# One attention and mixture-of-experts layer on one core: the map of whole tiles computed between other steps, turned a visit earlier, and ten fill addresses' registers read later

## What is computed

```python
x = L0_attn_x                                        # 32 x 256 x 128
h = _layernorm(x) * (1 + ca) + sa
x = x + ga * attention(h, w_in, b_in, w_out, b_out)  # 16 heads of 8
h = _layernorm(x) * (1 + cb) + sb
logits = h @ router_w                                # 14 experts
assignments = argmax(logits); weights = softmax(logits)[assignments]
hid = gelu(h @ w1[e] + b1[e]); out = hid @ w2[e] + b2[e]   # e = the token's expert
x = x + gb * out * weights
```

## Time and profile before

| | |
|---|---|
| median of the runs before | 603.12 us (three runs: 601.77, 603.12, 1474.33) |
| the profiled execution's own time | 602.05 us |
| its span, first to last instruction | 600.2 us |
| busy share of the span | PE 78%, DVE 92%, ACT 91%, POOL 81% |
| attention part, its drain and the expert part | about 0 to 490, 490 to 506 and 506 to 600 us |

### The profile page before, as it was taken

The page is one execution under the profiler, slowest core; times in us unless marked ns, Lnnn a source line. Parts: engine busy times, 40 slices in busy tenths (PEclk is TensorE's granted clock), DMA queues, the critical chain, the costliest instruction groups (busy, mean ns, idle before and its releaser), DMA issues.

```text
span 600.2 us, 12121 instructions
## 1 busy us (share of the span) xinstructions
PE 466.0 (78%) x2531; PEld 263.6 (44%) x2531; DVE 550.7 (92%) x1398; ACT 547.8 (91%) x2339; POOL 486.1 (81%) x647
## 2 busy tenths in 40 slices
PE   5456878887887887787787888778777677999993
PEld 2112433443443343343343343334333345889992
DVE  5899999999999999999999999999999977888994
ACT  2599999999999999999999999999999996678881
POOL 4566777989899988999999898999888687777773
PEclk9555565556556556756655655675665558999997
DMA  6366455544555554545455555666555513798760
GB/s 197 105 192 160 136 139 134 142 140 138 144 141 142 142 149 141 150 143 156 148 155 146 151 146 154 172 177 170 153 150 163 157 64 125 231 335 245 236 198 27
DMA packets 77080, 94.42 MB, mean 157 GB/s; under 512 B 12814, under 2 KB 60718, under 8 KB 77006
## 3 DMA queue, kind: packets, MB, share of 16 engines
q1 hardware_dynamic: 68850, 75.69, 45.7%
q0 software_dynamic: 6144, 16.82, 7.5%
q10 hardware_dynamic: 2015, 1.15, 0.8%
HBM read 58.41 MB, written 35.20 MB: 156 GB/s over the span
## 4 chain that ended last, share of the span: by engine, by line
ACT 44%; POOL 17%; PE 15%; DVE 8%; issue 7%; SPq 3%; DMA 3%; ACTq 1%; POOLq 0%; DVEq 0%
ACT scores L940 43%; PE scores L1263 5%; PE scores L1254 5%; POOL table L847 3%; DVE neg_max L1423 3%; SPq L592 3%; POOL xhat L792 2%; POOL rstd L775 2%; PE scores L1244 1%; POOL rest L581 1%; POOL parts L584 1%; POOL h_scaled L815 1%; DMA x_s<-table 1%; POOL att L804 1%; DMA more_rooms<-table 1%
## 5 line engine op out<-in xcount | busy, mean ns | idle before, releaser
L940 ACT ACTIVATE scores<-scores,neg_max 128x256 f32<-128x256 f32 x1024 | 467.2, 808 | 10.8 <-DVE neg_max L1423 10.6
L940 ACT ACTIVATION_READ_ACCUMULATOR scores<-scores,neg_max 128x1 f32 x1024 | 419.8, 569 | 0.0
L1423 DVE TENSOR_REDUCE neg_max<-scores 128x4 f32<-128x1024 f32 x256 | 309.3, 1211 | 7.4 <-PE scores L1104 6.8
L1104 PE MATMUL scores<-k_stack,q_stack 64*128 64x256 bf16 x1024 | 148.2, 388 | 79.6 <-ACT scores L940 65.5
L1104 PEld LDWEIGHTS scores<-k_stack,q_stack 64*128 64x128 bf16 x1024 | 34.1, 106 | 163.5 <-ACT scores L940 116.2
L847 POOL DMA_INDIRECT table<-rows,place_i x64 | 66.1, 1034 | 20.6 <-issue 15.2
L792 POOL TENSOR_SCALAR xhat<-rows,mv,rstd 128x128 f32<-128x128 f32 x60 | 47.6, 794 | 6.8 <-POOL rstd L775 6.8
L1263 PE MATMUL scores<-w_s,hid 128*128 x308 | 49.2, 284 | 1.4 <-DVE y_biased_s L1993 1.2
L1132 PE MATMUL side_a<-w_gated,opt_t 128*128 128x128 f32 x128 | 49.8, 491 | 0.0
L784 POOL TENSOR_SCALAR xhat<-x_s,mv,rstd 128x128 f32<-128x128 f32 x62 | 49.0, 798 | 0.4 <-POOL rstd L775 0.4
L906 POOL DMA_INDIRECT out_dram<-x_s x40 | 39.2, 980 | 12.2 <-issue 8.8
(11 more groups left out here) (230 smaller groups left out, 882.1 us busy)
## 6 DMA issues: line engine op xcount, KB each, us to landing
q_stack<-parts_dram SPq DMA_DIRECT2D x192, 64.0 KB, 2.9
x_s<-table SPq DMA_DIRECT2D x62, 192.5 KB
parts_dram<-parts SPq DMA_DIRECT2D x31, 384.0 KB
k_stack<-parts_dram SPq DMA_DIRECT2D x186, 64.0 KB, 2.3
mod_b<-mod_rows SPq DMA_DIRECT2D x32, 256.0 KB, 4.4
x_s<-in_x_dram SPq DMA_DIRECT2D x13, 256.0 KB, 5.1
table<-pad_tile SPq DMA_DIRECT2D x15, 192.5 KB
more_rooms<-table SPq DMA_DIRECT2D x15, 192.5 KB
```

Source lines behind the costliest of these rows:

```text
L940: last = act.activation(buf[:, k * L:k * L + L], buf[:, k * L:k * L + L], ACT.Exp, bias=neg_max[:, p, n:n + 1], accum_out=exp_sum[:, p, n: ...
L1104: last = pe.matmul(scores[:, c, at:at + L], q_stack[p][r, g + j, t * P:t * P + P], k_stack[p][r, g + j, :], start=True, stop=True)
L1423: dve.tensor_reduce(to, scores[:, (PAIRS * b.n + i) % RING, :].rearrange("p (e j m) -> p e j m", e=2, j=2), AX_X, ALU.max, negate=True).th ...
```

## The change

Three things change, and nothing of what is computed.

1. The map's twelve operations are split into functions of their own and stand one by one between the drain's last operations and the first `bias_y`, `gate_y` and `out_y`. Three of them (`map_rows_left`, `map_tiles`, `map_full`) now stand ahead of `bias_y(0)`.
2. `MAP_TURNED` is 7 and not 8: TensorE turns the map at the head of visit 7, and VectorE takes it in its own step 6.
3. SyncE reads the ten addresses of `end_row` behind the loads of visits 14 and 15.

```diff
-MAP_TURNED = 8
+MAP_TURNED = 7
...
                 sp.wait_ge(map_ready, 1)
                 whole_rows.extend(load_many(sp, tile_row, EARLY, whole_reload(EARLY), 0, PAD_AT))
-                ends.extend(load_many(sp, end_row, FILLS_FIRST, E - FILLS_FIRST, 0, PAD_AT))
...
                 sp.dma_start(rows_in[j % ROOMS][:, :], table[ds(row, P), :]).then_inc(rows_loaded[s], 16)
+                if j == FILLS_FROM - 1:
+                    ends.extend(load_many(sp, end_row, FILLS_FIRST, E - FILLS_FIRST, 0, PAD_AT))
...
                 note_ends()
+                map_rows_left()
                 own_place(other)
+                map_tiles()
                 note_place(other)
+                map_full()
                 weigh_last()
-                for n in range(FIRST):
-                    bias_y(n)
-                for n in range(FIRST):
-                    gate_y(n)
-                for n in range(FIRST):
-                    out_y(n)
-                map_counts()
+                bias_y(0)
+                bias_y(1)
+                map_spread()
+                gate_y(0)
+                map_below()
+                gate_y(1)
+                map_upto()
+                out_y(0)
+                map_bases()
+                map_from()
+                out_y(1)
+                map_in()
+                map_pick()
+                map_sums()
+                map_columns()
                 whole_y(FIRST)
-                map_rows()
-                map_columns()
                 bias_y(FIRST + 1)
                 gate_y(FIRST + 1)
```

Each new function holds one operation of the old chain, with a wait on the one that it reads:

```diff
-            def map_counts():
+            def map_rows_left():
 
                 dve.wait_ge(counted, GROUPS)
-                steps.then(dve.tensor_tensor(early_i[:, 0, :], next_row[0:NT, :], sums_of[:, 3, :], ALU.subtract))
...
+                step["left"] = steps.did(dve.tensor_tensor(early_i[:, 0, :], next_row[0:NT, :], sums_of[:, 3, :], ALU.subtract))
+
+            def map_tiles():
+
+                steps.after(step["left"])
```

43 lines of the change are left out of this document (31 added, 12 removed).

## The result

The changed kernel takes 604.31 us (median of 22 runs), the kernel before 603.12 us beside it: a ratio of 1.0027 with a 95% interval of 1.0016 to 1.0038, that is 1.0 to 2.3 us slower. It was timed again among the experiments and came out at 1.0039 (1.0027 to 1.0051). The forecast had the sign, and 0.84 us for a difference of 1.2 us by the two medians and 2.0 us by the mean of the two ratios; it stood on a base that was a microsecond too low, and it missed a second cost. The profiled execution took 604.24 us with a span of 602.4 us.

The account below looks back on a forecast made before the run. The prediction took TensorE to bound the expert part. From a base of 602.05 us, terms 1 and 2 gave 0, term 3's gain was used up inside term 4, and term 4 added 0.84: 602.9 us, range 601.4 to 604.2.

Parts of the forecast that it names:

- What bounds the kernel: TensorE bounds the expert part visit by visit; earlier rows could give back only visit 17's 0.32 us wait up to there.
- Term 1: Three map operations ahead of bias_y(0) make TensorE 0.16 us late, costing nothing while visit 17 still waits for rows.
- Term 2: VectorE's interleaved map is ready 1.6 us earlier, near 510.5; worth nothing on TensorE, where the turn's 0.29 us only moves.
- Term 3: SyncE's load 14 still waits for the last scatter, landing at 513.76; it goes out at 513.97, a 0.2 us gain.
- Term 4: SyncE's read of ten addresses, no longer covered, delays load 16 by 0.84 us, and visit 17's rows with it.
- The sum: From the profiled execution's 602.05 us, only the uncovered read's net 0.84 us counts and nothing hands it back: 602.9 us.
- Rows win: Earlier scatter landing or a 0.40 us read removes visit 17's wait for rows: 601.8 us, faster; chance 0.15.
- nothing arrives: The DMA engines' backlog absorbs the later load issue, visit 17's rows still land at 522: 602.1 us; chance 0.2.
- longer stretch: TensorE stays at 1.2 GHz for two more visits, costing 2.0 us: 603.8 us, slower; chance 0.1.

Follow-up runs that it names:

- e11: Kernel of e4 with the three map operations moved from ahead of bias_y(0) to behind it: 603.96 us, 1.0013 against the kernel before.
- e1: Changed kernel with the read of the ten addresses back at its old place, ahead of the wait for the scatters: 604.46 us, 1.0015 against the kernel before.
- e4: Changed kernel with the ten addresses read behind the first four fills, ahead of the wait for the map: 604.59 us, 1.0016 against the kernel before.
- e2: Kernel before with only the read of the ten addresses moved behind load 15: 604.85 us, 1.0016 against the kernel before.
- e16: Changed kernel, its read still late, with VectorE's steps in the order of e15: 604.52 us, 1.0022 against the kernel before.
- e5: Changed kernel with the read of the ten addresses made three times behind load 15: 605.61 us, 1.0033 against the kernel before.
- e15: Kernel of e11 with VectorE's output sums moved so that dependent map steps follow each other directly: 603.52 us, 0.9999 against the kernel before.
- e8: Changed kernel with six more copies of map_rows_left's operation, each waited for, ahead of bias_y(0): 605.65 us, 1.0032 against the kernel before.
- e7: Kernel of e4 with all fourteen fills late, from visit 22 on, none beside the last scatters: 604.82 us, 1.0021 against the kernel before.

## Why the prediction was wrong, by its steps

The time failed by its base: the sum started from 602.05 us where the kernel before takes 603.12, which is 1.07 of the 1.41 us of error. The difference between the kernels failed by the step on what bounds the kernel, which leaves one cost where the runs have two.

- **What bounds the kernel.** "So the expert part is TensorE's, visit by visit" is the step that failed. I never looked at GpSimd's groups of stores, which leave it some 2 us to spare in 84. Two stores less gain 0.7 us (interval 0.1 to 1.2) and a later row costs 0.5 (0 to 1.1), so GpSimd is at least close to being a second bound. That it is one is likely and not sure, since the first interval comes from an edit that also frees two loads and the second one reaches zero.
- **Term 1** was right in size (0.19 us for 0.16), and that it costs nothing agrees with e11, which has none of it and gains at most 0.2 us on e1 and e4, within their intervals. The section of the Trainium skill that the term sets against it, "The DRAIN you can't avoid" in "VectorE: DVE Perf Modes", also says that a next operation that is not held starts earlier. I left that out, and with it the starts 0.08 us apart are no contradiction.
- **Term 2.** The order of events was right, the map's end 0.4 us later than counted, the turn without a wait. Its conclusion that the turn's 0.29 us "only change place" for TensorE holds; what it left out is who else is hurt by a VectorE without gaps. The interleaving is the missing 0.8 to 1.0 us, most likely by way of the slow scatter. The term should have read the engines beside the interleaved stretch, not only those that wait for it by a semaphore. There was also a gain that I denied: TensorE's own "issue" stalls ahead of visits 14 and 16 are gone, with the turn of visit 16 at 519.50 where it was 520.51. Visit 17's wait for its rows takes it all back (its turn is at 522.35 and was at 522.03). So part of the longer wait is only TensorE arriving sooner.
- **Term 3** was right: landing at 513.79 for 513.76, load 14 at 514.00 for 513.97. But that is luck: the scatter's descriptors were written at 509.65 + 1.04 = 510.69, 1.4 us later than before, which the term did not have. The landing seems not to have moved with them. The trace of the kernel before doesn't show it, only that it came by 513.97; in e2, whose scatters are as quick, it is at 509.84 + 5.42 = 515.26, 6.76 us behind the start of the first of the two, and in the changed kernel 6.49 us.
- **Term 4** was right on SyncE and a little small: 1.07 us on load 16 for 0.84. From load 14 to load 16 SyncE took 516.65 - 514.00 = 2.65 us for the 2.45 that I summed, with 1.14 us for the read instead of 1.01; e2 and e16 have 1.0 and 1.3 us of time for it. That "nothing hands the 0.84 back" held in time for one read; e5 shows that more of the same isn't paid in full. Its path is not confirmed: visit 17 waits 1.91 and 1.78 us in e4 and e15 too, whose read is hidden.
- **The sum.** The forecast stands on 602.05 us, "the middle" of two runs and the profiled execution's own. All five medians of the kernel before, of 22 to 35 runs each, lie at 603.1 to 603.6. With the median shown, 603.12, the same terms give 604.0, 0.3 from the time measured, and a range to 605.3. Of the error of 1.41 us 1.07 are this base; the rest, 0.34 us, is that the difference was forecast as 0.84 us and is 1.2 us by the two medians (2.0 us by the mean of the two ratios). The range did not save it: it names the spread of 1.35 us between two runs, but its ends lie only 0.4 us outside the rivals' 601.8 and 603.8.
- **The rivals.** "Rows win" and "nothing arrives" are refuted by e2 and by the changed kernel's own ratios, the "longer stretch" by the granted clock, and no chance was given to a slower GpSimd. That the change stays within 2% held.

What stays open: which operation of VectorE keeps the scatter out (two SBUF inputs, or any; the 0.19 us of reduction in e11 lean to any), by which path each of the two costs reaches the end, and why a descriptor write that ends 1.4 us later does not seem to move the landing. None of this was tried.

## What to carry to other kernels

Sum an engine's operations with the fixed step between them before calling it free: 64 x (0.99 + 0.30) us filled all but some 2 of 84 us on GpSimd while its busy share there said 75%. Before filling the waits of a chain, look at what else runs beside it; the scatter ended about half a microsecond behind VectorE's first gap each time, and with two gaps kept on purpose no cost of the interleaving was left to measure (0.9999, 0.9986 to 1.0011). A wait that grows in the profile is not yet a cost: compare it with a kernel that has the wait and not the time. Set a forecast against the median of the runs, and keep the profiled execution for differences.

## What the runs showed of the hardware

GpSimd's indirect DMA, 0.96 to 1.03 us, takes 1.77 to 2.05 us beside a VectorE without gaps, and 1.06 with two gaps of 0.03 to 0.04 us; it ends 0.46 to 0.78 us behind the first gap. SyncE's read of ten registers varies with where it stands. Behind the wait for the map it took 0.95 us (e8) to 1.23 us (e5), 1.01 us before the change. Ahead of that wait, from 505.9 to 509.7 us, it took 1.45 us (e7, with no fill in front) to 1.85 us (e15, behind the first four fills; count, min/median/max ns):

```profile
L567 SPq TENSOR_LOAD <-end_row x2: 317/1082/1848, 506.6 to 509.0; - x2
```

I had expected the time of a register load to hang on the number of registers alone. What makes the early ones slower isn't shown.
